# Attention plus a routed expert layer: the sync queue of the expert stage reordered, and the gate and up weights of the next expert loaded in two parts

## The chip, the cores and the metric
The kernel runs on one core of one Trainium2 chip. The metric is the device time of one execution in microseconds (us). Before the change it was 9702.04 us, the median of three runs (9699.02 to 9710.63).

## What is computed
`x` has 16 x 512 = 8192 rows (tokens) of 1024 float32 values. A cross-attention block with a layernorm ahead of it is added to `x`, and then a routed expert layer with a layernorm ahead of it:

```python
routing_weights, selected_experts = top_k(softmax(x2d @ gate_kernel), 8)     # of 32 experts
w0 = ragged_dot(sorted_inputs, gate_proj, group_sizes)      # gate_proj: 32 x 1024 x 384
w1 = ragged_dot(sorted_inputs, up_proj, group_sizes)        # up_proj:   32 x 1024 x 384
inter = silu(w0) * w1
expert_out = ragged_dot(inter, down_proj, group_sizes)      # down_proj: 32 x 384 x 1024
output = sum over the 8 experts of a token of weight * expert_out
```

8192 tokens with 8 experts each give 65,536 rows of expert work. Everything is float32.

## The kernel before
Four stages follow one another: a setup, attention with the routing, a short schedule stage, and the experts (`experts_stage`), which the change touches. The schedule stage groups the rows by expert into **tiles** of up to 512 rows. Each tile belongs to one expert. An expert has several tiles in a row, and the last ones of an expert may be cut to 448 or 384 rows, so that its padding costs less. Here there are 144 tiles (`used`) of 32 experts. Below, "tile t" is the t-th of them, counted from 0, a **short** tile is one of 384 rows, and an expert's weights are loaded only at its first tile: every weight DMA of a later tile carries the condition `CHANGED`, which is 0 there, so it is issued but moves nothing.

Float32 precision comes from splitting each operand into a high and a low part (`..._hi`, `..._lo`) and making three matmuls for each product. For one tile TensorE (`products`) does:
- `gate_up(t, j)` for j = 0, 1, 2: 48 matmuls each (2 matrices, 8 slices c of the 1024 inputs, 3 products; L1576). At j = 0 it waits slice by slice for `xt_lo` (the low part of the input rows, DVE L1484), and before j = 0 and j = 1 for the output rows of the tile before to be out of the banks that it writes (`left_ready`, `right_ready`).
- `down(t, g)`: eight groups of 9 matmuls of 512 columns (L1599). Group g = 2q + n writes one half of output quarter q. The first two groups are done up to their last third while the third part of `h` is being made. In a short tile the two groups of the last quarter are a tiny matmul each (L1626). The last quarter's banks are those of quarter 0.

The other engines run one tile ahead for the weights. In PE's tile t,
- ACT and DVE split the weights of tile t+1 from the single raw buffer `gu_raw` as PE finishes with the old ones: `gate_up_hi(t+1, 0)` and `(t+1, 1)` after j = 1 of tile t, on DVE `gate_up_lo` of the same two (L1490); `(t+1, 2)` only after `left_rows(t, 0)` on ACT and `right_rows(t, 0)` on DVE, which stand ahead of them in program order;
- `left_rows(t, q)` (ACT L1428) and `right_rows(t, q)` (DVE L1514) scale the output rows of quarter q by the routing weight and take them out of PSUM. The one of q = 0 waits for `entry_kept`: the routing weights and row numbers of tile t in `entry_now`. Behind them stand, on both engines, the third weight part, the splitting of the next tile's rows (`x_hi` L1403, `x_lo` L1484) and the later quarters;
- POOL gathers rows for tile t+2 (L1363), then scatters the rows of tile t (L1375).

Program order on ACT after j = 1 of a tile:

```python
gate_up_hi(t, 0); gate_up_hi(t, 1); silu(t - 1, 2)
left_rows(t - 1, 0)
gate_up_hi(t, 2)
for c in range(DC):
    x_hi(t, c)
    if c in ROWS_AFTER:                      # (0, 2, 5)
        left_rows(t - 1, 1 + ROWS_AFTER.index(c))
```

DVE has the same order with `gate_up_lo`, `right_rows` and `x_lo`.

All weights and all table entries are loaded by SyncE, in one order, through one hardware DMA queue. Its four loads are `load_entries(t)` (which rows to gather, `entry_in`, 4 DMAs, L1276), `load_gate_up(t)` (3 MB in 8 DMAs, L1311, after `gulo_ready` says that all three parts of tile t-1 are split), `load_rows(t)` (`entry_now` of tile t, 8 small DMAs, L1287 and L1295, after the scatters of tile t-1 have landed) and `load_down(t)` (1.5 MB in one DMA, L1318, after `dlo_ready` says that the down weights of tile t-1 are split). Before the change the loop runs them as entries(t), gate and up(t-1), rows(t-2), down(t-1).

Of the kernel before, what the change touches and what calls it, by code (L numbers as in the profile page):

```python
# [24 lines left out]
P = 128  # L25
# [11 lines left out]
def wait(eng, sem, value):  # L37

    if isinstance(value, int) and value <= 0:
        return  # L40
    eng.wait_ge(sem, value)  # L41
# [1144 lines left out]
def experts_stage(nc, sb, sem, banks, sched_row, tiles_over, xn_dram, table, gate_proj, up_proj, down_v, out, *,  # L1186
# [12 lines left out]
    QUAD = 32  # L1199
    KQ = P // QUAD  # L1200
# [7 lines left out]
    with mem:  # L1208
        gu_raw = sb(mem, "gu_raw", [P, 2, DC, M], F32)
# [19 lines left out]
        GU_BANK = banks[0:6]  # L1229
        D_BANK = (banks[6:8], banks[0:2], banks[2:4], banks[6:8])  # L1230

        ROWS_AFTER = (0, 2, 5)
        PAIRS = RUNS // 2
        assert PAIRS == DC
# [2 lines left out]
        GATHER_AT = tuple(range(9, GATE_PACES + 1, 3)) + tuple(GATE_PACES + n for n in (2, 4, 5))  # L1237
        assert len(GATHER_AT) == RUNS

        gu_loaded, d_loaded, entry_loaded = sem("gu_loaded"), sem("d_loaded"), sem("entry_loaded")  # L1240
        gathered, scattered = [sem(f"gathered{n}") for n in range(PAIRS)], sem("scattered")
        pace = sem("pace")
        quarter_made, rows_made, entry_kept = sem("quarter_made"), sem("rows_made"), sem("entry_kept")
# [1 line left out]
        guhi_ready, gulo_ready, dhi_ready, dlo_ready = sem("guhi_ready"), sem("gulo_ready"), sem("dhi_ready"), sem("dlo_ready")  # L1245
# [17 lines left out]
        def _(sp):  # L1263
            def hold(semaphore, value):

                sp.wait_ge(semaphore, value)
                sp.sem_inc(fence["sp"], 1)

            def scheduled(t, word, most):
                return sp.value_load(sched_row[0:1, bass.ds(SCHED_WORDS * t + word, 1)], min_val=0, max_val=most)  # L1270

            def load_entries(t):
                first_row = scheduled(t, FIRST_ROW, TABLE_PAD)
                wait(sp, rows_made, t)
                for k in range(KQ):
                    sp.dma_start(entry_in[k * QUAD:(k + 1) * QUAD, :, :].rearrange("r (e m) two -> r e (m two)", m=2),  # L1276
                                 table[bass.ds(first_row, SLOT_ROWS), :].rearrange("(e r m) two -> r e (m two)", r=QUAD, m=2)
                                 ).then_inc(entry_loaded, 16)
# [20 lines left out]
            def expert_of(t):  # L1299

                e = sp.value_load(sched_row[0:1, bass.ds(SCHED_WORDS * t + EXPERT, 1)], min_val=0, max_val=E - 1)
                first = isinstance(t, int) and t == 0
                only = {} if first else {"cond": sp.value_load(sched_row[0:1, bass.ds(SCHED_WORDS * t + CHANGED, 1)], min_val=0, max_val=1)}
                return e, only

            def load_gate_up(t):
                e, only = expert_of(t)
                wait(sp, gulo_ready, MC * t)
                for n, w in enumerate(weights_v):
                    for k in range(KQ):  # L1310
                        sp.dma_start(gu_raw[k * QUAD:(k + 1) * QUAD, n, :, :],  # L1311
                                     w[bass.ds(e, 1), k, :, :, :].rearrange("e r c m -> r (e c) m"), **only
                                     ).then_inc(gu_loaded, 16)

            def load_down(t):
                e, only = expert_of(t)
                wait(sp, dlo_ready, MC * t)
                sp.dma_start(d_raw[:, :, :], down_v[bass.ds(e, 1), :, :, :].rearrange("e p c d -> p (e c) d"), **only  # L1318
                             ).then_inc(d_loaded, 16)

            def tile(t):
                load_entries(t)
                load_gate_up(t - 1)
                load_rows(t - 2)
                load_down(t - 1)
                hold(d_loaded, 16 * t)

            used = used_tiles(sp)
            load_entries(0)
            load_gate_up(0)  # L1330
            load_entries(1)
            load_down(0)
            tile(2)
            tiles_from(sp, 3, used, tile)
            load_entries(used)
            load_gate_up(used - 1)
            load_rows(used - 2)
            load_down(used - 1)
            load_rows(used - 1)
            hold(d_loaded, 16 * used)  # L1340
            hold(entry_loaded, 16 * KQ * (used + 1))
            hold(entry_kept, 16 * 2 * KQ * used)

# [55 lines left out]
        def _(act):  # L1399
# [5 lines left out]
            def gate_up_hi(t, j):  # L1405

                cols = slice(j * P, (j + 1) * P)
                act.wait_ge(gu_loaded, 16 * 2 * KQ * (t + 1))
                wait(act, gu_done, MC * (t - 1) + j + 1)
                act.activation(gu_hi[:, :, :, cols], gu_raw[:, :, :, cols].rearrange("p n c m -> p c n m"), ACT.Copy  # L1410
                               ).then_inc(guhi_ready, 1)
# [19 lines left out]
            def tile(t):  # L1431
# [9 lines left out]
                for c in range(DC):  # L1441
                    x_hi(t, c)
                    if c in ROWS_AFTER:
                        left_rows(t - 1, 1 + ROWS_AFTER.index(c))

            used = used_tiles(act)
# [16 lines left out]
        def _(dve):  # L1463
# [53 lines left out]
            def tile(t):  # L1517
# [18 lines left out]
                for c in range(DC):  # L1536
                    x_lo(t, c)
                    if c in ROWS_AFTER:
                        right_rows(t - 1, 1 + ROWS_AFTER.index(c))

# [126 lines left out]
```

## Time and profile before

| what | value |
|---|---|
| median of three runs | 9702.04 us |
| the profiled execution, span from first to last instruction | 9705.4 us |
| PE busy | 9157.1 us (94%) |
| DVE, ACT, POOL busy | 6503.2, 4465.8, 5282.3 us |
| DMA queue q0 (POOL's gathers and scatters) | 604.72 MB |
| DMA queue q1 (SyncE's) | 308.44 MB |
| mean granted TensorE clock | 0.974 |

The profiled execution has no time of its own apart from its span, 9705.4 us, which is 3.4 us over the median of the runs and inside their spread. The first 3.08 ms are setup, attention and schedule, and the rest, some 6.6 ms, are the 144 tiles. Busy times say how long an engine worked, and only the waits and the order of events say which of them set the end.

### The profile page before, as it was taken

How to read it: one execution, taken by the hardware profiler on the slowest of the kernel's cores; microseconds unless marked ns; L12 is line 12 of the kernel's file. 1: busy time of each engine (PE TensorE's matmuls, PEld its weight loads, DVE VectorE, ACT ScalarE, POOL GpSimd, SP SyncE). 2: the span in 40 equal slices, each digit the busy share in tenths (PEclk: the TensorE clock that was granted, in tenths of full speed). 3: DMA queues.
4: the chain of work that ended last, by engine and by line, in shares of the span. 5: the costliest groups of instructions: out<-in, count | busy, mean ns of one | idle time of the engine just before them, and what ended most of it. 6: DMA issues, size and time to landing. Idle time of an engine off the chain costs nothing.

```text
span 9705.4 us, 172457 instructions
## 1 busy us (share of the span) xinstructions
PE 9157.1 (94%) x44592; PEld 7702.0 (79%) x44593; DVE 6503.2 (67%) x10304; ACT 4465.8 (46%) x7458; POOL 5282.3 (54%) x5081
## 2 busy tenths in 40 slices
PE   7898898898895999999999999999999999999999
PEld 5776777677774888888888888888888888888888
DVE  7888888888885566666655656666666566656565
ACT  6676666676673333333333333333333333333333
POOL 3444444444445566565655656555666555655564
PEclk8999999999997999999999999999999999999999
DMA  2111111111112555555544655555555455555554
GB/s 88 48 53 49 50 51 49 51 53 48 49 51 72 108 112 132 113 112 117 112 106 106 137 109 110 118 111 125 118 112 111 106 118 108 134 109 111 114 123 80
DMA packets 664527, 918.18 MB, mean 95 GB/s; under 512 B 338193, under 2 KB 477457, under 8 KB 663954
## 3 DMA queue, kind: packets, MB, share of 16 engines
q0 software_dynamic: 209920, 604.72, 29.2%
q1 hardware_dynamic: 454162, 308.44, 12.2%
q8 instruction: 168, 2.75, 0.1%
q14 instruction: 277, 2.27, 0.1%
HBM read 1064.79 MB, written 376.45 MB: 148 GB/s over the span
## 4 chain that ended last, share of the span: by engine, by line
PE 60%; DMA 3%; issue 3%; DVE 2%; ACT 1%; SPq 1%; POOL 0%; DVEq 0%; ACTq 0%; POOLq 0%
PE bank L1576 39%; PE bank L1599 21%; DMA gu_raw<-in_L_ffn_up_proj 3%; SPq L1311 1%; DVE gu_lo L1490 0%; ACT xT_hi L1403 0%; DVE xT L1479 0%; ACT gu_hi L1410 0%; DVE h L1502 0%; DVE d_lo L1495 0%; DVE h_lo L1507 0%; DVE h_hi L1505 0%; DVE xT_lo L1484 0%; POOL xg L1363 0%; DVEq L41 0%
## 5 line engine op out<-in xcount | busy, mean ns | idle before, releaser
L1363 POOL DMA_INDIRECT xg<-xn_rows,gather_row x2304 | 2766.7, 1201 | 2086.7 <-PE bank L1576 1310.6
L1576 PE MATMUL bank<-xT_hi,gu_hi 128*128 128x512 f32 (+2 forms) x6912 | 2553.4, 369 | 102.8 <-DVE xT_lo L1484 94.5
L1576 PE MATMUL bank<-xT_lo,gu_hi 128*128 128x512 f32 (+2 forms) x6912 | 2543.2, 368 | 0.0
L1576 PE MATMUL bank<-xT_hi,gu_lo 128*128 128x512 f32 (+2 forms) x6912 | 2543.1, 368 | 0.0
L1421 ACT ACTIVATE gated<-bank 128x512 f32<-128x512 f32 x432 | 258.2, 598 | 3030.0 <-PE bank L1576 2740.1
L1576 PEld LDWEIGHTS bank<-xT_hi,gu_hi 128*128 128x128 f32 x6912 | 1299.2, 188 | 278.6 <-issue 91.5
L1375 POOL DMA_INDIRECT out_rows<-rows_out,entry_now x576 | 1129.0, 1960 | 671.6 <-DVE rows_out L1514 322.5
L1576 PEld LDWEIGHTS bank<-xT_lo,gu_hi 128*128 128x128 f32 x6912 | 1299.7, 188 | 158.9
L1576 PEld LDWEIGHTS bank<-xT_hi,gu_lo 128*128 128x128 f32 x6912 | 1299.1, 188 | 158.9
L1502 DVE TENSOR_TENSOR h<-bank,gated 128x512 f32<-128x512 f32 x432 | 297.6, 689 | 1578.5 <-ACT gated L1421 1133.8
L1599 PE MATMUL bank<-d_hi,h_hi 128*128 128x512 f32 x3162 | 1257.3, 398 | 76.7 <-DVE h_lo L1507 76.7
L1599 PE MATMUL bank<-d_lo,h_hi 128*128 128x512 f32 x3162 | 1244.6, 394 | 0.0
L1599 PE MATMUL bank<-d_hi,h_lo 128*128 128x512 f32 x3162 | 1244.4, 394 | 0.0
L1490 DVE TENSOR_TENSOR gu_lo<-gu_raw,gu_hi 128x2048 fp32r<-128x2048 f32 x432 | 973.3, 2280 | 251.0 <-ACT gu_hi L1410 136.0
L480 ACT ACTIVATE probs<-bank,neg_max 128x512 f32<-128x512 f32 x1024 | 704.9, 688 | 716.6 <-DVE neg_max L605 670.6
L1410 ACT ACTIVATE gu_hi<-gu_raw 128x2048 fp32r<-128x2048 f32 x432 | 809.1, 1907 | 185.3 <-DMA gu_raw<-in_L_ffn_up_proj 171.3
L1514 DVE TENSOR_SCALAR rows_out<-bank,entry_now 128x512 f32<-128x512 f32 x576 | 431.3, 749 | 680.3 <-PE bank L1599 664.8
L1428 ACT ACTIVATE rows_out<-bank,entry_now 128x512 f32<-128x512 f32 x576 | 395.6, 687 | 1003.6 <-PE bank L1599 851.5
L1599 PEld LDWEIGHTS bank<-d_hi,h_hi 128*128 128x128 f32 x3162 | 602.0, 190 | 249.0 <-issue 128.9
L619 DVE TENSOR_TENSOR pT_lo<-bank,pT_hi 128x512 fp32r<-128x512 f32 x1024 | 693.1, 677 | 136.3 <-ACT pT_hi L488 109.8
L605 DVE TENSOR_REDUCE neg_max<-bank 128x1 f32<-128x512 f32 x1024 | 700.6, 684 | 122.4 <-issue 44.3
L1479 DVE STREAM_TRANSPOSE xT<-xg 128x512 f32<-128x512 f32 x1152 | 747.5, 687 | 0.0
(162 smaller groups left out, 14769.3 us busy)
## 6 DMA issues: line engine op xcount, KB each, us to landing
gu_raw<-in_L_ffn_gate_proj SPq DMA_DIRECT2D x576, 384.0 KB
gu_raw<-in_L_ffn_up_proj SPq DMA_DIRECT2D x576, 384.0 KB
d_raw<-in_L_ffn_down_proj SPq DMA_DIRECT2D x144, 1536.0 KB
xg<-xn_rows,gather_row POOLq DMA_INDIRECT x2304
x_t<-in_x SPq DMA_DIRECT2D x64, 512.0 KB, 4.4
inv_wide<-inverse_sums SPq DMA_DIRECT2D x512, 64.0 KB
out_rows<-x SPq DMA_DIRECT2D x64, 512.0 KB, 5.0
xn_rows<-xn SPq DMA_DIRECT2D x64, 512.0 KB
```

The costliest lines, as they stand in the source:

```text
L480: act.activation(probs[h % 4][:, :], S_BANK[h % 2][:, :], ACT.Exp, bias=neg_max[:, h:h + 1], accum_out=row_sum[:, h:h + 1]).then_inc(exp_r ...
L605: dve.tensor_reduce(neg_max[:, h:h + 1], S_BANK[h % 2][:, :], AX.X, ALU.max, negate=True).then_inc(max_ready, 1)
L619: dve.tensor_tensor(pT_lo[g % 2][:, :, k, :], PT_BANK[h % 2][:, :].rearrange("p (c t) -> p c t", c=TC), pT_hi[g % 2][:, :, k, :].bitcast(F ...
L1363: pool.indirect_dma_start(out=xg[:, m, :], out_offset=None, in_=quarter_rows, in_offset=bass.IndirectOffsetOnAxis(ap=gather_row[:, m:m + 1 ...
L1375: pool.indirect_dma_start(out=out, out_offset=bass.IndirectOffsetOnAxis(ap=entry_now[:, q, 0:1], axis=0), in_=rows_out[:, q, :], in_offset ...
L1410: act.activation(gu_hi[:, :, :, cols], gu_raw[:, :, :, cols].rearrange("p n c m -> p c n m"), ACT.Copy).then_inc(guhi_ready, 1)
L1428: act.activation(rows_out[:, q, 0:512], D_BANK[q][0][:, :], ACT.Copy, scale=entry_now[:, q, 1:2].bitcast(F32)).then_inc(left_ready, 1)
L1479: dve.transpose(xT[:, :, 2 * pair * QUAD:2 * (pair + 1) * QUAD].rearrange("p c (m r) -> p m c r", r=QUAD), xg[:, 2 * pair:2 * pair + 2, :] ...
L1490: dve.tensor_tensor(gu_lo[:, :, :, cols], gu_raw[:, :, :, cols].rearrange("p n c m -> p c n m"), gu_hi[:, :, :, cols].bitcast(F32), ALU.su ...
L1514: dve.tensor_scalar(rows_out[:, q, 512:1024], D_BANK[q][1][:, :], entry_now[:, q, 1:2].bitcast(F32), None, ALU.mult).then_inc(right_ready, 1)
L1576: last = nc.tensor.matmul(bank[:, 0:cols], w[:, c, n, j * P:(j + 1) * P], v[:, c, 0:cols], start=(c == 0 and w is gu_hi and v is xT_hi), s ...
L1599: last = nc.tensor.matmul(D_BANK[q][n][:, 0:cols], v[:, k, q * P:(q + 1) * P], w[:, k, n * 512:n * 512 + cols], start=(k == ks[0] == 0 and ...
```

## The change
On SyncE the loop body now runs entries(t+1), down(t-1), the first part of gate and up(t), rows(t-2), the second part of gate and up(t). The first part is columns 0 to 255 of both matrices (j = 0 and 1) and waits only until the first two parts of tile t-1 are split. The second is columns 256 to 383 (j = 2) and waits for all three. Each part has its own semaphore, and ACT waits for the one that it needs. Each part has 8 DMAs, so a tile has 16 where it had 8. Rows of 1536 bytes become rows of 1024 and 512 bytes. The start and the end of the queue are rewritten to fit. PE, DVE, ACT and POOL keep their order.

```diff
+        EARLY = MC - 1
+        GU_PARTS = (slice(0, EARLY * P), slice(EARLY * P, M))
...
-        gu_loaded, d_loaded, entry_loaded = sem("gu_loaded"), sem("d_loaded"), sem("entry_loaded")
+        gu_loaded, d_loaded, entry_loaded = (sem("gu_early"), sem("gu_late")), sem("d_loaded"), sem("entry_loaded")
...
-            def load_gate_up(t):
+            def load_gate_up(t, part):
+
                 e, only = expert_of(t)
-                wait(sp, gulo_ready, MC * t)
+                wait(sp, gulo_ready, MC * t if part else MC * (t - 1) + EARLY)
                 for n, w in enumerate(weights_v):
                     for k in range(KQ):
-                        sp.dma_start(gu_raw[k * QUAD:(k + 1) * QUAD, n, :, :],
-                                     w[bass.ds(e, 1), k, :, :, :].rearrange("e r c m -> r (e c) m"), **only
-                                     ).then_inc(gu_loaded, 16)
+                        sp.dma_start(gu_raw[k * QUAD:(k + 1) * QUAD, n, :, GU_PARTS[part]],
+                                     w[bass.ds(e, 1), k, :, :, GU_PARTS[part]].rearrange("e r c m -> r (e c) m"), **only
+                                     ).then_inc(gu_loaded[part], 16)
...
             def tile(t):
-                load_entries(t)
-                load_gate_up(t - 1)
+                load_entries(t + 1)
+                load_down(t - 1)
+                load_gate_up(t, 0)
                 load_rows(t - 2)
-                load_down(t - 1)
-                hold(d_loaded, 16 * t)
+                load_gate_up(t, 1)
+                hold(d_loaded, 16 * (t - 1))
 
             used = used_tiles(sp)
             load_entries(0)
-            load_gate_up(0)
+            for part in range(2):
+                load_gate_up(0, part)
             load_entries(1)
             load_down(0)
-            tile(2)
+            load_entries(2)
+            for part in range(2):
+                load_gate_up(1, part)
+            load_entries(3)
+            load_down(1)
+            load_gate_up(2, 0)
+            load_rows(0)
+            load_gate_up(2, 1)
             tiles_from(sp, 3, used, tile)
...
             def gate_up_hi(t, j):
 
                 cols = slice(j * P, (j + 1) * P)
-                act.wait_ge(gu_loaded, 16 * 2 * KQ * (t + 1))
+                act.wait_ge(gu_loaded[0 if j < EARLY else 1], 16 * 2 * KQ * (t + 1))
```

The order of SyncE before, in the loop: the end of the table loads of one tile, the down weights, and the end of the pass. L1303 is part of `expert_of`, L1295 of `load_rows`, L1318 of `load_down`.

```order
L1295 DMA entry_now<-slot_table 32x2
L1301 TENSOR_LOAD sched_row
L1301 ISA x2
L1303 TENSOR_LOAD sched_row
L1303 ISA x2
L1318 ISA [waits dlo_ready]
L1318 DMA d_raw<-in_L_ffn_down_proj 128x3x1024
L1266 REGISTER_ALU
L1256 UNCONDITIONAL_BRANCH [waits d_loaded]
```

Here nothing that waits for a weight split of the following tile stands ahead of the table loads of tile t-2: they come before the down weights of tile t-1 and before the pass that loads gate and up of tile t.

The order of SyncE now, at the same loads: L1314 is `load_gate_up`, here its first part for tile t, and L1289 is `load_rows` of tile t-2.

```order
L1314 DMA gu_raw<-in_L_ffn_gate_proj 32x8x256
L1314 DMA gu_raw<-in_L_ffn_up_proj 32x8x256 x4
L1272 ISA
L1272 TENSOR_LOAD sched_row
L1272 ISA x2
L41 REGISTER_ALU
L1289 ISA [waits scattered]
L1289 DMA entry_now<-slot_table 32x3x2
```

The table loads of tile t-2 have moved behind the down weights of tile t-1, the entries of tile t+1 and the 8 DMAs of the first part of tile t.

The wait ahead of that first part on SyncE now (L1321 is `load_down`, L1305 part of `expert_of`):

```order
L1321 ISA [waits dlo_ready]
L1321 DMA d_raw<-in_L_ffn_down_proj 128x3x1024
L1303 ISA
L1303 TENSOR_LOAD sched_row
L1303 ISA x2
L1305 ISA
L1305 TENSOR_LOAD sched_row
L1305 ISA x2
L41 REGISTER_ALU
L1314 ISA [waits gulo_ready]
L1314 DMA gu_raw<-in_L_ffn_gate_proj 32x8x256
```

So whatever stands behind `[waits gulo_ready]`, the table loads among it, cannot be issued before the second part of tile t-1 is split.

## Rows read from the trace of the kernel before
**Rows 1.** The page: the chain that ended last, share of the span by engine.

```profile
PE 60%; DMA 3%; issue 3%; DVE 2%; ACT 1%; SPq 1%; POOL 0%; DVEq 0%; ACTq 0%; POOLq 0%
```

**Rows 2.** Waits from 3200 us on: who <- for whom: us in total, times, longest.

```profile
PE bank L1599 <- DVE h_lo L1507: 70.3, 18, 6.2
```

**Rows 3.** Chain of waits, a full tile and a change of expert: start us, us, what.

```profile
4154.77 32.64 PE bank L1576 x144
...
4281.32 23.64 DMA gu_raw<-in_L_ffn_up_proj
```

**Rows 4.** Timeline of PE there: start us, us, what [idle before <- releaser].

```profile
4313.41 0.61 PE L1599 MATMUL bank<-d_hi,h_hi 128*128 128x512 f32 x1 [4.45 <-DVE h_lo L1507]
...
4317.35 0.39 PE L1599 MATMUL bank<-d_lo,h_hi 128*128 128x512 f32 x1
```

**Rows 5.** First gate matmul of tiles 25, 26 and 27: timeline of PE.

```profile
4241.48 0.39 PE L1576 MATMUL bank<-xT_hi,gu_hi 128*128 128x384 f32 x1
...
4280.10 0.39 PE L1576 MATMUL bank<-xT_hi,gu_hi 128*128 128x384 f32 x1
...
4324.78 0.45 PE L1576 MATMUL bank<-xT_hi,gu_hi 128*128 128x512 f32 x1
```

**Rows 6.** Table loads and gate/up loads on SyncE: timeline, tiles 25 and 26.

```profile
4253.04 1.87 SPq L1287 DMA_DIRECT2D entry_now<-slot_table  x4
4255.76 2.50 SPq L1295 DMA_DIRECT2D entry_now<-slot_table  x4
...
4276.58 2.11 SPq L1311 DMA_DIRECT2D gu_raw<-in_L_ffn_gate_proj  x4
4278.78 6.46 SPq L1311 DMA_DIRECT2D gu_raw<-in_L_ffn_up_proj  x4
...
4320.17 1.16 SPq L1311 DMA_DIRECT2D gu_raw<-in_L_ffn_gate_proj  x4
4321.42 0.90 SPq L1311 DMA_DIRECT2D gu_raw<-in_L_ffn_up_proj  x4
```

**Rows 7.** Short tile 25: timeline of DVE, and of ACT (the last row).

```profile
4262.96 4.45 DVE L1490 TENSOR_TENSOR gu_lo<-gu_raw,gu_hi 128x2048 fp32r<-128x2048 f32 x2
...
4273.95 2.35 DVE L1490 TENSOR_TENSOR gu_lo<-gu_raw,gu_hi 128x2048 fp32r<-128x2048 f32 x1 [1.06 <-issue]
4276.82 0.74 DVE L1514 TENSOR_SCALAR rows_out<-bank,entry_now 128x512 f32<-128x512 f32 x1
4277.48 1.28 DVE L1484 TENSOR_TENSOR xT_lo<-xT,xT_hi 128x512 fp32r<-128x512 f32 x2
...
4271.42 0.69 ACT L1428 ACTIVATE rows_out<-bank,entry_now 128x512 f32<-128x512 f32 x1 [3.19 <-issue]
```

**Rows 8.** Full tile 23: DVE, ACT, and the first matmul of tile 24.

```profile
4180.22 4.45 DVE L1490 TENSOR_TENSOR gu_lo<-gu_raw,gu_hi 128x2048 fp32r<-128x2048 f32 x2
...
4191.23 0.69 ACT L1428 ACTIVATE rows_out<-bank,entry_now 128x512 f32<-128x512 f32 x1 [3.19 <-PE bank L1599]
...
4203.83 0.33 PE L1576 MATMUL bank<-xT_hi,gu_hi 128*128 128x384 f32 x1
```

**Rows 9.** First use of a small load: timeline of SyncE, then DVE.

```profile
3042.74 2.75 SPq L1276 DMA_DIRECT2D entry_in<-slot_table  x4
...
3052.16 8.99 SPq L1276 DMA_DIRECT2D entry_in<-slot_table  x4
...
3046.89 0.23 DVE L1471 TENSOR_SCALAR gather_row<-entry_in,quarter_no 128x16 int32<-128x16 int32 x1 [9.61 <-DMA entry_in<-slot_table]
```

**Rows 10.** Stretches: us, busy of PE, PEld, DVE, ACT, POOL, PEclk, DMA share, GB/s.

```profile
4267.40:4276.30 8.90, 8.90 (x40) 7.09 (x39) 4.93 (x7) 5.23 (x7) 7.07 (x7) 1.00 0.29 89
4301.00:4312.00 11.00, 7.96 (x42) 7.10 (x41) 5.71 (x5) 4.20 (x3) 7.18 (x7) 1.00 0.94 282
4313.60:4317.00 3.40, 3.40 (x9) 2.62 (x9) 0.63 (x1) 1.94 (x2) 0.00 (x0) 0.50 0.17 5
```

**Rows 11.** Gate/up matmuls of the short tiles, grouped by shape.

```profile
L1576 PE MATMUL bank<-xT_hi,gu_hi 128*128 128x384 f32 x2352 | 794.5, 338 | 12.2 <-DVE xT_lo L1484 12.2
```

More of the change, by code:

```diff
@@ L1321, in tile @@
             def tile(t):
-                load_entries(t)
-                load_gate_up(t - 1)
+                load_entries(t + 1)
+                load_down(t - 1)
+                load_gate_up(t, 0)
                 load_rows(t - 2)
-                load_down(t - 1)
-                hold(d_loaded, 16 * t)
+                load_gate_up(t, 1)
+                hold(d_loaded, 16 * (t - 1))
             used = used_tiles(sp)
             load_entries(0)
-            load_gate_up(0)
+            for part in range(2):
+                load_gate_up(0, part)
             load_entries(1)
             load_down(0)
-            tile(2)
+            load_entries(2)
[6 more added lines that the diff above has]
+            load_gate_up(2, 1)
             tiles_from(sp, 3, used, tile)
-            load_entries(used)
-            load_gate_up(used - 1)
+            load_down(used - 1)
             load_rows(used - 2)
-            load_down(used - 1)
             load_rows(used - 1)
             hold(d_loaded, 16 * used)
+            for part in range(2):
+                hold(gu_loaded[part], 16 * 2 * KQ * used)
             hold(entry_loaded, 16 * KQ * (used + 1))
```

## The prediction
> **What bounds the kernel now.** I read the page first: the chain that ended last is PE for 60% of the span, and the only DMA in it is the load of gate and up weights [rows 1]. PE is the bound, so what counts is where PE stands still. The waits from 3200 us on show one cause: PE waits for the last part of `h` in 18 places, 70.3 us in all [rows 2]. The chain at one of them shows why [rows 3]: the gate and up weights of the next expert land at 4304.96, ACT can only then split them, its `silu` and DVE's `h` stand behind that, and PE gets going at 4313.41 after 4.45 us of standing still [rows 4]. Then it is slow for a while: a matmul is recorded with 0.61 us where later ones have 0.39, and the granted clock in that stretch is 0.50, so 1.2 instead of 2.4 GHz, after the engine stood still [rows 4, 10]. Tile 26, where this happens, lasts 44.68 us, and the equally short tile 25 ahead of it 38.62 [rows 5]. So one stall costs 6.1 us where its gap is 4.45. The 70.3 us of gaps cost about 70.3 x 6.1 / 4.45 = 96 us, and the starts of all tiles added up give 102. I take 100 us: all that an earlier load of the weights can bring back in the steady part.
>
> **What the first part gains.** The load starts at 4276.58 today, 0.28 us after the third `gu_lo` ends at 4276.30, and with the change it may start after the second, at 4267.41, 9.2 us sooner and with 2 MB instead of 3 [rows 6, 7]. Today it lands at 4304.96 and that is about 6 us late, so it is first wanted near 4299. Today 3 MB take 28.4 us from first issue to landing (4276.58 to 4304.96 [rows 3, 6]). Two thirds of that, 19 us, would be 4286.6. The second part is used after the next `left_rows`, 17 us later. Both are hidden: **-100 us**. At the start of the stage the first split waits for 2 MB instead of 3. But gathers end it a few us later anyway, so I take -4 us there (bounds 0 and -9, a third of the 28.4 us).
>
> **What is moved past what.** The price is on the other loads of that queue. `load_rows(t-2)`, the 8 small DMAs that ACT and DVE need before they may take output rows out, was issued early in its tile (4253.04, used at 4271.42 [rows 6, 7]). Now it stands behind `gulo_ready` of the first part and behind that part's 8 DMAs. Both lie within the same tile. Counted from the end of the second `gu_lo` (G):
>
> - Tiles where the following weights do not change: 0.28 us from G to the first issue, 2.15 for 8 issues that move nothing (4320.17 to 4322.32), 0.85 for the table look-up that precedes a load (4254.91 to 4255.76), 5.22 for the 8 small issues (4253.04 to 4258.26), 1.4 from the last issue to first use, as DVE shows it (3045.49 to 3046.89) [rows 6, 9]. Sum: **G + 9.9**.
> - Tiles before a change: the 8 DMAs are real and the small ones queue behind 2 MB. Rows 9 show small loads held up behind weights: 4 issues take 8.99 us where they usually take under 3. DMA was 0.29 busy in the 8.9 us after G and moved 282 GB/s when full [rows 10], so 2 MB at 0.7 x 282 = 197 GB/s take 10.6 us. With about 1 us to the first byte, 1.4 to use and another for the small packets this gives **G + 14**. The lower bound is the issue alone, 0.28 + 4.3 + 0.85 + 5.22 + 1.4 = 12.1. With today's slow issue (8.65 us) it is 16.4, and with today's rate for the whole load (19 us) about 20.6.
>
> When is it wanted? In short tile 25 `left_rows` starts at 4271.42, which is G + 4.0 [rows 7]. In full tile 23 it is G + 6.6 (4184.67 to 4191.23 [rows 8]); for a tile of 448 rows I take G + 5.4, between the two. So **every** tile gets its rows late: by 5.9, 3.3 or 4.5 us without a weight change, by 10.0, 7.4 or 8.6 with one.
>
> What of this reaches PE? Behind `left_rows(t, 0)` stand the third weight split, `x_lo` of slice 0 and the second `right_rows`, which ends 6.14 us later (4277.56), and PE may not start the next tile before. In tile 25 it starts at 4280.10, a slack of 2.5 us. In full tile 23 the same point leaves 6.5 us (4191.23 + 6.14 = 4197.4, start 4203.83) [rows 5, 7, 8]. After that point DVE still has 5.9 us of work to the last slice (7 slices at 0.64, 2 `right_rows` at 0.74 [rows 7]), while PE gets to that slice after 21 matmuls, 4.8 us at 0.23 (32.64 / 144 [rows 3]) or 3.6 at 0.17, that is 384/512 of it. The delay that is free is therefore slack + 4.8 (3.6) - 5.9:
>
> - Full tile without a weight change: free up to 5.4 (full tile next) or 4.2 (short next), delay 3.3: **0**. For 448 rows 4.5 against 4.2: 0.3 in 7 tiles, 2 us.
> - Short tile without a weight change. There are 49 short tiles (2352 matmuls of that shape, 48 in each tile [rows 11]). 22 of them are the last of an expert, with a full tile next: 5.9 - 1.4 = 4.5 us each, **99 us**. 10 have another short tile next: 5.9 - 0.25 less the 0.95 that a short tile after a short one loses already (38.62 against 37.65, from 4203.83 to 4241.48 [rows 5, 8]), 4.7 each, **47 us**.
> - Tiles before a weight change (31, by the lengths of the blocks): 15 short before short, 10.0 - 0.25 - 0.95 = 8.8 and 0.5 for the slow clock after a gap of 7.5 us, which is mostly hidden since DVE sets the pace there: **140 us**. 5 of 448 before short, 8.6 - 4.2 = 4.4: **22 us**. 11 full ones, 7.4 against 5.4, 4.8 or 4.2 by what follows (4, 5, 2 of them): 8 + 13 + 6 = **27 us**.
>
> New stalls: 2 + 99 + 47 + 140 + 22 + 27 = 337 us. The rest costs nothing: eight more issues a tile (2.15 us) and the entries and down weights that move ahead lie on SyncE, which issues for some 10 us of a tile's 38.6 and otherwise waits, as it does for `gu_lo` until 4276.58 [rows 5, 6]. Without that cover it would be 144 x 2.15 = 310 us. The scatters start some 2 to 7 us later behind POOL's gathers, whose rows are used most of a tile later.
>
> Sum against the profiled span: 9705.4 - 100 - 4 + 337 = 9938. That execution stands 3.4 us over the median, so I predict 9702 + 233 = **9935 us**.
>
> A rule of the Trainium skill is weighed here. In the trace, with gathers, scatters and weights at once, 3 MB take 28.4 us, 111 GB/s of the 282 that the engines reach [rows 3, 6, 10]. DMA: Bandwidth & Descriptors, section Queues, rings and completion order, says that each DMA engine takes turns between the queues by packets, and reads one ring in order. By it the weights could get less than the 0.7 that I give them beside gathers, and the sum would then be that of the third rival, 10,138 us.
>
> **The rivals.**
> 1. *The table rows are not late, and the change does what it is for.* Were small DMAs not held by the weights, or `gu_lo` of part two early enough, only -104 would be left: 9702 - 104 = 9598 us, faster. For it: the weight stall is real and goes in full. It decides if the small loads are usable by G + 4 to 6.5. Against it: 2.15 + 0.85 + 5.22 us of issue after G are 8.2 already without any queueing. 0.04. A neighbouring rule: the same section of DMA: Bandwidth & Descriptors says that completion is not in order within an issuing engine. By it small DMAs might finish before the weights do, but they are issued no sooner.
> 2. *A draw.* The rows are late, but the tiles before a weight change are no worse than others: 31 delays fall to those of the first list. Then new stalls are 99 + 47 + 2 + 15 x 4.7 + 2 = 221 us, and 9819 us is still slower. A draw needs 32 + 15 short tiles to lose 2.2 us each instead of 4.5 to 9. The gap at their start alone is 5.9 - 2.5 = 3.4. 0.03.
> 3. *The weights go as slowly as today.* G + 20.6 in 31 tiles, 6.6 us more each: +205, 10,138 us. For it: contention with gathers. Against it: today's load runs beside the scatters, and these now wait for the rows themselves. 0.06.
> 4. *Half of the price*, 9819 us as worked out under 2, the weight changes no worse than other tiles: 0.08.
>
> **The numbers.** The forecast has 0.79, the rivals 0.04, 0.03, 0.06 and 0.08. Its own bounds: landing at 12.1 and 9.0 instead of 14 and 9.9 gives 337 - 57 - 29 = 251, 9849 us; issue at 16.4 gives +74, 10,009 us. The range reaches down to the second rival's 9819 and up by some clock loss: 9815 to 10,040. A measurement of this kernel tells 0.2% (19 us) from no change. Slower 0.93, within 0.2% 0.03, faster 0.04.
>
> **What would show it.** Right: PE no longer waits for `h_lo` at L1599 in the steady part; ACT `rows_out` (L1440 now) waits for a DMA of `entry_now` in nearly every tile; PE waits for `xT_lo` or the output rows at the first gate matmul, about 3.4 us after each short tile and 7 us before a weight change; short tiles last 42 to 48 us instead of 38, full ones stay at 49.2; the clock shows more stretches of 0.5, at tile starts. Wrong: `rows_out` of quarter 0 starts within 4 to 6.6 us of the second `gu_lo`, as before, or PE waits for weights still.

## The result and the profile after

The changed kernel takes 10,069.12 us (median of 5 runs, 10,060.24 to 10,073.94) against 9702.04, a ratio of 1.0375 with a 95% interval of 1.0363 to 1.0388. It is 367 us slower. The prediction had 9935 us, +233, and a range up to 10,040. The direction and the mechanism came out as forecast, the size did not, and the time lies above the range.

The first place to look is the list of waits of the changed kernel from 3200 us on (who <- for whom: us in total, times, longest).

```profile
ACT rows_out L1440 <- DMA entry_now<-slot_table: 1201.2, 129, 16.1
DVE rows_out L1526 <- DMA entry_now<-slot_table: 956.1, 129, 14.2
...
PE bank L1588 <- DVE rows_out L1526: 220.8, 55, 5.1
...
PE bank L1638 <- ACT rows_out L1440: 70.3, 15, 5.0
...
PE bank L1611 <- ACT rows_out L1440: 40.8, 16, 3.6
...
PE bank L1588 <- DVE xT_lo L1496: 11.1, 28, 0.5
```

ACT and DVE now wait for the table rows in 129 tiles. Before, no such row was among the waits. PE's wait for `h_lo` (18 times, 70.3 us [rows 2]) is gone. In its place PE waits 55 times for output rows at the start of a tile, 15 times ahead of the tiny matmul of a short tile's last quarter, and 16 times ahead of the last quarter of a longer one: 345 us of standing still where it was 86. The page's chain has changed with it:

```profile
PE 43%; issue 10%; DVE 6%; SPq 5%; DMA 3%; ACT 2%; DVEq 0%; POOL 0%; ACTq 0%; POOLq 0%
PE bank L1588 31%; PE bank L1611 12%; DMA entry_now<-slot_table 2%; DVE gu_lo L1502 2%; SPq L1314 2%; ACT gu_hi L1422 1%; DVE xT L1491 1%; SPq L1272 1%; SPq L1289 1%; DVE rows_out L1526 1%; SPq L1297 1%; DVE d_lo L1507 1%; DVE xT_lo L1496 1%; DVE h_hi L1517 0%; ACT gated L1433 0%
```

PE's part is down from 60% [rows 1] to 43%, and the queue of SyncE (SPq) stands in it with 5%.

Short tile 25 again, whose second next tile has a new expert. First SyncE's timeline in the changed kernel, for this tile (from 4327) and for tile 24 ahead of it (from 4282), where the weights do not change:

```profile
4282.92 1.14 SPq L1314 DMA_DIRECT2D gu_raw<-in_L_ffn_gate_proj  x4
4284.15 0.88 SPq L1314 DMA_DIRECT2D gu_raw<-in_L_ffn_up_proj  x4
4286.53 1.86 SPq L1289 DMA_DIRECT2D entry_now<-slot_table  x4
4289.45 2.65 SPq L1297 DMA_DIRECT2D entry_now<-slot_table  x4
...
4327.37 2.11 SPq L1314 DMA_DIRECT2D gu_raw<-in_L_ffn_gate_proj  x4
4329.57 1.88 SPq L1314 DMA_DIRECT2D gu_raw<-in_L_ffn_up_proj  x4
4332.48 1.84 SPq L1289 DMA_DIRECT2D entry_now<-slot_table  x4
4335.29 2.38 SPq L1297 DMA_DIRECT2D entry_now<-slot_table  x4
```

DVE's timeline, the same two tiles:

```profile
4278.18 4.45 DVE L1502 TENSOR_TENSOR gu_lo<-gu_raw,gu_hi 128x2048 fp32r<-128x2048 f32 x2
...
4322.63 4.45 DVE L1502 TENSOR_TENSOR gu_lo<-gu_raw,gu_hi 128x2048 fp32r<-128x2048 f32 x2
...
4343.94 0.75 DVE L1526 TENSOR_SCALAR rows_out<-bank,entry_now 128x512 f32<-128x512 f32 x1 [14.13 <-DMA entry_now<-slot_table]
...
4349.26 0.74 DVE L1526 TENSOR_SCALAR rows_out<-bank,entry_now 128x512 f32<-128x512 f32 x1
```

And ACT's, for the first use of the rows in tile 24 and in tile 25:

```profile
4293.32 0.69 ACT L1440 ACTIVATE rows_out<-bank,entry_now 128x512 f32<-128x512 f32 x1 [9.87 <-PE bank L1611]
...
4343.93 0.69 ACT L1440 ACTIVATE rows_out<-bank,entry_now 128x512 f32<-128x512 f32 x1 [16.03 <-DMA entry_now<-slot_table]
```

The second `gu_lo` ends at 4282.63 and 4327.08. That is G. The rows are used at G + 10.7 in tile 24 and at G + 16.9 in tile 25, where it was G + 4.0 [rows 7]. In tile 25 the last small DMA is issued by 4337.67, 6.3 us before that use, and it waits behind the weights: by the times of the single packets in the trace, the first packet of a table row moves at 4340.93, when all but the last of the weights have moved (they end at 4341.64), and the last one ends at 4341.88. It is so in all 31 tiles before a weight change: 93 to 98% of the weight packets start ahead of the first table packet. Over all tiles the first use lies at G + 16.4 to 17.1 in these 31 (median 16.6), at G + 10.3 to 11.3 in other tiles of 384 and 448 rows (median 10.8), and at G + 9.7 to 10.1 in other full ones (median 9.8). Only tile 142, at the rewritten end of the queue, has its rows at G + 4.0. PE after that, in its timeline:

```profile
4344.67 0.69 PE L1638 MATMUL bank<-d_hi,h_hi 128*128 128x128 f32 x2 [4.91 <-ACT rows_out L1440]
4350.29 0.68 PE L1588 MATMUL bank<-xT_hi,gu_hi 128*128 128x384 f32 x1 [4.93 <-DVE rows_out L1526]
4350.77 0.53 PE L1588 MATMUL bank<-xT_lo,gu_hi 128*128 128x384 f32 x1
...
4356.48 0.33 PE L1588 MATMUL bank<-xT_hi,gu_lo 128*128 128x384 f32 x1
```

Two gaps of 4.9 us, and then slow matmuls. By its first matmuls (4299.64 and 4350.29) tile 25 lasts 50.7 us; before it lasted 38.6 [rows 5]. The stretches of the same kernel: the first is that of the weights' transfer, the second that of the slow matmuls (us, busy of PE, PEld, DVE, ACT, POOL, PEclk, DMA share, GB/s).

```profile
4328.30:4341.60 13.30, 11.46 (x50) 8.89 (x48) 1.44 (x3) 0.00 (x0) 5.13 (x5) 1.00 1.07 217
...
4350.30:4356.00 5.70, 5.70 (x18) 5.70 (x19) 5.70 (x11) 4.83 (x7) 4.47 (x3) 0.50 1.07 212
```

The clock records after 3200 us hold 376 us at 0.50 (1.2 GHz) in 55 stretches, where it was 93 us in 18.

What each kind of tile lasts more than before, from the starts of all 144 tiles (so for the first 143):

| tiles | number | us more each | us in all |
|---|---|---|---|
| short, before a weight change | 15 | 11.25 | 168.7 |
| 448 or 512 rows, before a weight change | 16 | 4.3 | 69.0 |
| short, last of its expert | 22 | 1.19, on top of the 102.4 us of weight stalls that are gone | 26.2 |
| full, first of its expert | 31 | 1.50 (2.11 in the 22 behind a short tile, 0.02 in the other 9) | 46.6 |
| short, others | 11 | 4.34 | 47.7 |
| all others | 48 | about 0.2 | 10.4 |

Together 368.7 us. Of the last row 9.1 us lie in 9 tiles of 448 and 512 rows that are the last of an expert. With the 102.4 us that came back, the new stalls are 471 us, where the prediction had 337.

### The profile page after: what moved, and what is told of

It is laid out like the page before. It is cut to its first block, busy times and chain, and to the rows that moved or that the text cites. A ratio compares the mean times of both kernels' runs of the same rounds, so it can differ in the third digit from the quotient of the medians.

```text
span 10071.9 us, 176762 instructions
## 1 busy us (share of the span) xinstructions
PE 9252.4 (92%) x44592; PEld 7763.5 (77%) x44593; DVE 6474.7 (64%) x10304; ACT 4436.6 (44%) x7458; POOL 5108.5 (51%) x5081
## 4 chain that ended last, share of the span: by engine, by line
PE 43%; issue 10%; DVE 6%; SPq 5%; DMA 3%; ACT 2%; DVEq 0%; POOL 0%; ACTq 0%; POOLq 0%
PE bank L1588 31%; PE bank L1611 12%; DMA entry_now<-slot_table 2%; DVE gu_lo L1502 2%; SPq L1314 2%; ACT gu_hi L1422 1%; DVE xT L1491 1%; SPq L1272 1%; SPq L1289 1%; DVE rows_out L1526 1%; SPq L1297 1%; DVE d_lo L1507 1%; DVE xT_lo L1496 1%; DVE h_hi L1517 0%; ACT gated L1433 0%
## 5 line engine op out<-in xcount | busy, mean ns | idle before, releaser
L1375 POOL DMA_INDIRECT xg<-xn_rows,gather_row x2304 | 2735.4, 1187 | 1960.7 <-PE bank L1588 1303.1
L1588 PE MATMUL bank<-xT_hi,gu_hi 128*128 128x512 f32 (+2 forms) x6912 | 2600.8, 376 | 324.8 <-DVE rows_out L1526 222.2
L1588 PE MATMUL bank<-xT_lo,gu_hi 128*128 128x512 f32 (+2 forms) x6912 | 2581.7, 374 | 0.0
L1588 PE MATMUL bank<-xT_hi,gu_lo 128*128 128x512 f32 (+2 forms) x6912 | 2579.3, 373 | 0.0
L1588 PEld LDWEIGHTS bank<-xT_hi,gu_hi 128*128 128x128 f32 x6912 | 1327.6, 192 | 522.4 <-DVE xT_lo L1496 261.0
L1387 POOL DMA_INDIRECT out_rows<-rows_out,entry_now x576 | 991.2, 1721 | 1334.5 <-DVE rows_out L1526 1219.7
L1588 PEld LDWEIGHTS bank<-xT_lo,gu_hi 128*128 128x128 f32 x6912 | 1327.6, 192 | 161.4
L1588 PEld LDWEIGHTS bank<-xT_hi,gu_lo 128*128 128x128 f32 x6912 | 1325.3, 192 | 164.0
```

What stands on the lines that cost most here:

```text
L1375: pool.indirect_dma_start(out=xg[:, m, :], out_offset=None, in_=quarter_rows, in_offset=bass.IndirectOffsetOnAxis(ap=gather_row[:, m:m + 1 ...
L1387: pool.indirect_dma_start(out=out, out_offset=bass.IndirectOffsetOnAxis(ap=entry_now[:, q, 0:1], axis=0), in_=rows_out[:, q, :], in_offset ...
L1588: last = nc.tensor.matmul(bank[:, 0:cols], w[:, c, n, j * P:(j + 1) * P], v[:, c, 0:cols], start=(c == 0 and w is gu_hi and v is xT_hi), s ...
```

## The experiments

Every ratio below is of runs on the same chip to the kernel before, which took 9693 to 9710 us (medians) in these comparisons.

**1. The rows put ahead.** The order of the changed kernel with one line moved, in the loop and in the start:

```diff
                 load_down(t - 1)
-                load_gate_up(t, 0)
                 load_rows(t - 2)
+                load_gate_up(t, 0)
                 load_gate_up(t, 1)
```

> The changed kernel with one move: the table loads of tile t-2 stand ahead of the first part of gate and up, not behind it. Theory (the late table rows are the whole loss, the two-part load is the gain): the rows are in time again, PE no longer waits for weights, about 9600 us (9702 - 100 - 4). Rival A (the loads themselves cost: 16 DMAs of 1024 and 512 bytes for 8 of 1536, started beside the gathers): the time stays over 9800 us although the rows are in time. Rival B (both, in part): between 9620 and 9800 us.

Measured: 9596.3 us, ratio 0.989 (0.9873 to 0.9906). Of PE's waits from 3200 us on only these are left:

```profile
PE bank L1588 <- DVE xT_lo L1496: 12.2, 26, 0.5
PE bank L1588 <- issue: 0.2, 1, 0.2
```

The rows are used at G + 4.0 in short and 6.6 in full tiles, as before the change; in tile 25, whose second `gu_lo` ends at 4238.34, on ACT:

```profile
4242.34 0.69 ACT L1440 ACTIVATE rows_out<-bank,entry_now 128x512 f32<-128x512 f32 x1 [3.18 <-PE bank L1611]
```

So the place of this one load makes all of the loss, some 470 us, and the rest of the change is a gain of 1.1%. Rival A, that the loads themselves cost, is out. SyncE's timeline of tile 25 shows how rows and weights both come in time:

```profile
4224.62 1.83 SPq L1289 DMA_DIRECT2D entry_now<-slot_table  x4
4227.31 2.63 SPq L1297 DMA_DIRECT2D entry_now<-slot_table  x4
4238.64 2.13 SPq L1314 DMA_DIRECT2D gu_raw<-in_L_ffn_gate_proj  x4
4240.86 1.88 SPq L1314 DMA_DIRECT2D gu_raw<-in_L_ffn_up_proj  x4
4247.52 2.11 SPq L1314 DMA_DIRECT2D gu_raw<-in_L_ffn_gate_proj  x4
4249.72 6.61 SPq L1314 DMA_DIRECT2D gu_raw<-in_L_ffn_up_proj  x4
```

The rows go out 14 us ahead of the first part of the new expert's weights, which starts 0.3 us after its `gu_lo`. The second part follows at 4247.52, and its last four issues take 6.61 us, where those of the first part took 1.88. Nothing that is due soon stands behind them.

**2. The split in the old order.** Against the kernel before, the loop alone (the start and the end of the queue are changed to match):

```diff
             def tile(t):
                 load_entries(t)
-                load_gate_up(t - 1)
+                load_gate_up(t - 1, 0)
+                load_gate_up(t - 1, 1)
                 load_rows(t - 2)
                 load_down(t - 1)
                 hold(d_loaded, 16 * t)
```

> The old order of the sync queue, entries(t), gate and up(t-1), rows(t-2), down(t-1), with gate and up loaded in the two parts of the change. Theory: the split alone brings the whole gain, since the rows of a tile still stand ahead of the weights two tiles on: about 9600 us, as rows_first. Rival A (small pieces cost): over 9700 us. Rival C (the gain needs the down weights to be loaded ahead): only part of the 100 us comes, 9640 us or more, with waits for d_raw or gu_raw left.

Measured: 9597.1 us, ratio 0.9897 (0.988 to 0.9913), with 13 us of PE waits left:

```profile
PE bank L1584 <- DVE xT_lo L1492: 12.2, 26, 0.5
...
PE bank L1584 <- DVE rows_out L1522: 1.0, 1, 1.0
```

The split alone brings the whole gain. Rival C is out: nothing of it needed the down weights ahead. Here the table rows of tile t-2 do stand behind both parts of the weights of tile t-1, and it does no harm, because these weights were let go a tile earlier: those of tile 27 are issued from 4232.30 on, the rows of tile 26 behind them from 4259.09 on, and their first use is at 4274.60. So what hurts is not any large load ahead, but one that is let go shortly before the small one is due.

**3. The new order alone,** rows ahead, weights whole:

```diff
             def tile(t):
-                load_entries(t)
-                load_gate_up(t - 1)
-                load_rows(t - 2)
+                load_entries(t + 1)
                 load_down(t - 1)
-                hold(d_loaded, 16 * t)
+                load_rows(t - 2)
+                load_gate_up(t)
+                hold(d_loaded, 16 * (t - 1))
```

> The new order with the rows put ahead of the weights, and gate and up whole, 8 DMAs of 1536-byte rows, after the old wait for all three parts. Theory: the load starts when it did before (third gu_lo), so nothing is gained or lost: 9702 us within 15, with the 18 waits for h_lo as before. Rival C (the earlier down weights take the weight load's way or clear it): more than 20 us away from 9702 to either side.

Measured: 9717.3 us, ratio 1.0021 (1.0012 to 1.0031). The waits for `h_lo` are all there:

```profile
PE bank L1602 <- DVE h_lo L1510: 79.8, 21, 5.8
```

The theory said 9702 within 15. The median lies 15.3 above that, and against the kernel before on the same chip the ratio makes it 12 to 30 us, so the theory missed by a little, and rival C (over 20 us away) is neither met nor out. 21 waits of 79.8 us in all instead of 18 of 70.3 [rows 2] are 9.5 us of it; the tiles' starts put 12.9 us more into the tiles, 10 of them in the short last tiles of an expert. Why three more waits arise was not looked into. The new order gains nothing by itself.

**4. The wait without the queueing.** The rows go out after the wait for the second `gu_lo`, but ahead of the eight DMAs:

```diff
                 e, only = expert_of(t)
                 wait(sp, gulo_ready, MC * t if part else MC * (t - 1) + EARLY)
+                if rows_of is not None:
+                    load_rows(rows_of)
                 for n, w in enumerate(weights_v):
```

The loop and the start pass the tile of the rows to this function in place of their own call of `load_rows`.

> The changed kernel, but the rows are issued right after the wait for the second gu_lo and ahead of the 8 DMAs of the first part. So they keep the wait and lose the queueing behind 2 MB and the 2.15 us of issues. Theory: rows usable at G + 7.7 us in all tiles; 3.7 us late in short tiles, whose gap at the next tile's start is then 1.2 us, too short for the clock to fall; 22 x 2.3 + 25 x 2.5 = 113 us of new stall, 9598 + 113 = 9711 us, and at most 5 stretches of half clock after 3200 us. Rival (the wait alone makes the loss, whatever is queued ahead): near 10069 us. Rival (only the 2 MB ahead matter): near 9600 us.

Measured: 9695.2 us, ratio 0.9998 (0.9988 to 1.0008). Waits from 3200 us on:

```profile
ACT rows_out L1440 <- DMA entry_now<-slot_table: 756.4, 139, 7.6
...
DVE rows_out L1526 <- DMA entry_now<-slot_table: 492.3, 139, 5.7
...
PE bank L1588 <- DVE rows_out L1526: 50.9, 47, 1.9
```

The rows are used at G + 7.4 to 8.4 in short tiles, median 7.5 (7.7 expected). PE's 47 waits are those of 47 short tiles, 1.1 us each (1.2 expected), and only 2 stretches of half clock are left. This kernel takes 99 us more than experiment 1, where 113 were expected. So the wait costs about 100 us, which is what the split gains, and what stands between the wait and the rows (the eight issues, their bytes and a table look-up) costs the other 374. Both rivals, the wait alone (10,069) and the 2 MB alone (9600), are out.

**5. and 6. Without the bytes.** In the kernel before and in the changed one, gate and up are loaded for tile 0 alone. Later DMAs are issued and move nothing:

```diff
-            def expert_of(t):
+            def expert_of(t, changed_at=None):
...
-                only = {} if first else {"cond": sp.value_load(sched_row[0:1, bass.ds(SCHED_WORDS * t + CHANGED, 1)], min_val=0, max_val=1)}
+                only = {} if first else {"cond": sp.value_load(sched_row[0:1, bass.ds(SCHED_WORDS * (t if changed_at is None else changed_at) + CHANGED, 1)], min_val=0, max_val=1)}
...
             def load_gate_up(t):
-                e, only = expert_of(t)
+                e, only = expert_of(t, 1)
```

The condition is then always that of tile 1, which is 0, so all tiles compute with the gate and up weights of the first expert. The down weights are loaded as before.

> The kernel before, with gate and up loaded for tile 0 only: the DMAs of later tiles are issued but move nothing (all tiles use the first expert's gate and up weights, so that part of the computation is changed). Theory (the stalls for these weights cost 100 us, gap and slow clock together): 9602 us, and no wait for h_lo after 3200 us. Rival: only the gaps count, 70 us: 9632 us.

> The changed kernel, with gate and up loaded for tile 0 only, in the same way (that part of the computation is changed). It takes the queueing behind 2 MB away and leaves the wait and 8 issues. Theory: rows usable at G + 10 us in all tiles, 47 short tiles lose 4.4 us each and 22 full tiles behind them 1.9 more for the slow clock: 9602 + 207 + 42 = 9851 us. Rival (only the weights' bytes ahead of the rows hurt): near 9602 us. Rival (the clock plays no part): 9602 + 207 = 9809 us or less.

Measured: 9604.5 us for the kernel before, ratio 0.9894 (0.9877 to 0.991), and 9895.9 us for the changed one, ratio 1.0198 (1.0179 to 1.0216). The first has no wait for `h_lo` left. Of PE's waits from 3200 us on there are only these:

```profile
PE bank L1576 <- DVE xT_lo L1484: 12.2, 26, 0.5
PE bank L1576 <- issue: 3.4, 1, 3.4
```

So the weight stalls cost 9702 - 9604 = 98 to 106 us (against its own comparison of 9710). The gaps alone, 70 us, are not enough. The second shows what the wait and eight issues cost without any bytes of these weights: 9896 - 9604 = 291 us. Its waits:

```profile
ACT rows_out L1440 <- DMA entry_now<-slot_table: 1115.8, 139, 10.9
...
PE bank L1588 <- DVE rows_out L1526: 213.8, 47, 5.1
```

47 short tiles with 4.5 us of gap each. In its tiles of 448 and 512 rows nothing is lost except in the first of an expert. The bytes are worth the rest, 10,069 - 9896 = 173 us. By the starts of tiles 155 of it lie in the 31 tiles before a weight change and 9 in the longer tiles behind them. The changed kernel without these bytes came 45 us above the 9851 expected: the full tiles behind short last ones lose 44 us together, near the 42 expected, and the short tiles 5.5 us each and not 4.4. The rival of the bytes alone (9602) is out. That of no part for the clock (9809 or less) cannot be judged by this number, since the excess lies in the short tiles; the next experiment tries it.

**7. The clock held up.** The changed kernel with 8 more matmuls ahead of the last quarter and 8 at the end of a short tile, out of constant operands into a free bank:

```diff
+                def filler():
+                    for _ in range(8):
+                        nc.tensor.matmul(GU_BANK[2 * MC - 2][:, :], fill_r[:, 0:P], fill_r[:, :],
+                                         start=True, stop=True)
...
+                        if g == OUT_GROUPS - NH:
+                            filler()
                         empty_group(t, g)
+                if cols == LESS_TWO:
+                    filler()
```

> The changed kernel with 16 matmuls of 512 columns more in each short tile, into a free bank, with operands of their own: 8 ahead of the wait for the last quarter's banks, 8 at the tile's end. They take 3.6 us of PE where PE stands still for 4 to 13 us, and add no wait. Theory (after gaps over some 3.3 us the clock falls, and that is the term I set too low, 283 us more at half clock than before): half-clock stretches after 3200 us fall from 55 to 25 or fewer, and the time by 50 to 110 us, to 9960 to 10,020 us. Rival (the slow clock is hidden behind DVE's slices, and the loss is later landings alone): the stretches fall and the time stays at 10,069 within 15 us, or rises.

Measured: 10,041.6 us, ratio 1.034 (1.0322 to 1.0357), 27.5 us less than the changed kernel (34 by the ratios). The gaps at the starts of tiles shrink, as they should:

```profile
PE bank L1596 <- DVE rows_out L1531: 63.2, 52, 3.3
```

The half-clock stretches fall from 55 to 30 (25 or fewer expected) and their time from 376 to 160 us, but the gain is half of the least that I expected. 216 us less of half clock are worth 27.5 us, one eighth, where a PE that is bound by its own work would get back one half. The tiles say why. The first 48 matmuls of tile 27, which stands behind a short last tile, in the changed kernel and in this one (the columns of the stretches above):

```profile
4395.00:4408.50 13.50, 13.49 (x48) 10.94 (x49) 11.24 (x17) 4.89 (x7) 7.27 (x5) 0.80 0.81 138
```

```profile
4382.60:4394.30 11.70, 11.56 (x48) 8.96 (x49) 11.26 (x17) 4.92 (x7) 7.97 (x5) 1.00 0.88 144
```

In the 22 such tiles the 49th matmul starts 13.05 us after the first, and 11.69 us with the filler. This is 1.4 us each, and their loss falls from 2.11 to 0.75 us, 30 us in all.

In 10 short tiles behind a short one, all at full clock with the filler, it starts after 10.14 us instead of 10.62: 0.5 us each. There DVE's last `x_lo` slice is ready 5.3 us after the tile's first matmul at either clock. PE is there to use it after 5.4 us at full clock and after 5.9 in the changed kernel, so DVE's pace hides most of the slow clock. The short tiles as a whole lose as much as before or a little more (11.20 against 11.25 before a weight change, 4.90 against 4.34 before another short one). That does not prove their clock to be free, for two reasons. Their rows are used 0.3 to 0.4 us later after G with the filler (16.9 and 11.1 against 16.6 and 10.8, why was not tried), which eats the gain. And the boundaries behind the 15 short tiles before a weight change keep much of their half clock (6.8 us each instead of 11.2).

So neither theory stands as it was put: the clock has a price, 30 us behind short last tiles and an estimated 12 at the starts of short tiles (0.5 us in 25), and it is the smaller part of the loss.

**8. Half of the bytes ahead.** The rows are issued between the gate and the up DMAs of the first part:

```diff
                 for n, w in enumerate(weights_v):
+                    if n == 1 and rows_of is not None:
+                        load_rows(rows_of)
                     for k in range(KQ):
```

The loop and the start pass the tile of the rows, as in experiment 4.

> The changed kernel with the rows issued between the 4 gate and the 4 up DMAs of the first part: 1 MB ahead of them instead of 2. Theory (the rows wait for the bytes issued ahead of them): 1 MB drains in half of the 13.3 us, so the issues and the bytes end together, rows usable at about G + 10.5 us before a weight change (16.6 with 2 MB) and at G + 9 elsewhere, where 4 issues are saved. Every short tile then loses some 4 us, which is 9840 us within 30. Rival (the rows are held until the whole load has landed, however little stands ahead): G + 16 to 17 before a weight change, and 10,000 us or more.

Measured: 9873.9 us, ratio 1.0185 (1.0167 to 1.0202), 34 us above the 9840 expected and 4 outside its bounds. The rows are used at G + 11.1 to 12.2 before a weight change and at G + 8.9 to 10.6 in the other tiles (10.5 and 9 expected). SyncE's timeline of tile 25, before a weight change (its second `gu_lo` ends at 4279.32), and DVE's first use of the rows:

```profile
4279.61 2.10 SPq L1316 DMA_DIRECT2D gu_raw<-in_L_ffn_gate_proj  x4
4283.22 1.60 SPq L1289 DMA_DIRECT2D entry_now<-slot_table  x4
4285.68 2.91 SPq L1297 DMA_DIRECT2D entry_now<-slot_table  x4
4288.69 1.84 SPq L1316 DMA_DIRECT2D gu_raw<-in_L_ffn_up_proj  x4
```

```profile
4290.85 0.75 DVE L1526 TENSOR_SCALAR rows_out<-bank,entry_now 128x512 f32<-128x512 f32 x1 [8.80 <-DMA entry_now<-slot_table]
```

The last small DMA is issued by 4288.59, its last packet ends 0.85 us later, and DVE begins at 4290.85. Over the 31 tiles the last table packet ends 0.85 us (median) after the last issue, where it was 3.9 us in the changed kernel. So the issues and not the bytes now set it. The first table packet moves when 43 to 50% of the weights have moved. Nothing holds the rows until the whole load has landed. What is issued ahead of them is what they wait for.

## Why the prediction was right in kind and wrong in size

**Right.** The bound and the gain: 100 us of weight stalls, measured 98 to 106 (experiment 5) and 102.4 by tiles, gone in full. That the rows of each tile become late, and that this costs more than the split gains: experiments 1 and 4 show it directly. The delay in full tiles without a weight change (G + 9.9, measured 9.8; the 31 that are neither first nor last of an expert are within 0.04 us of before), the 448-row ones (0), and the short ones before another short one (4.7 predicted, 4.34 measured, in 11 tiles and not 10). All four rivals are out: the faster case, the draw and the half price by more than 240 us, and the third by 70, since the rows came at G + 16.6 and not 20.6. Two slips in the rivals changed nothing: the third adds up to 10,140, and the 221 us of the second and fourth are two thirds of 337 and not half. The 4 us at the start of the stage stay open: tile 0 began between 3065 and 3079 us in the traces of the kernels here, with the same stages ahead of it, and that hides them.

**Wrong, first step: "2 MB at 0.7 x 282 = 197 GB/s take 10.6 us ... this gives G + 14".** The transfer took 13.3 us, 158 GB/s, while all queues together moved 217, and the use came at G + 16.6. So the share of 0.7 was right (158 of 217 is 0.73), and the total was not. The 282 was read from a stretch in which 1.57 of 3.10 MB were down weights, in packets of 4096 bytes, while the first part of gate and up now moves in packets of 1024. After 3200 us such a packet took 80 ns on average in the changed kernel, one of 1536 bytes 100 ns in the kernel before, and one of 4096 bytes (down weights) 166 ns in the changed kernel and 183 in the one before: 12.8, 15.4 and 22 to 25 bytes per ns. That the packet size is the cause was not tried by itself; the gathers beside them differ too. The 2 MB were 2048 packets, as many as the 3 MB had been.

The upper bound with today's slow issue, 16.4, happened to be near it, for another reason: the issues took 4.1 us and not 8.65, and the transfer made it late. The bytes cost 173 us by experiment 6, where the prediction's own terms give 189 - 15 x 4.7 - 2 = 117. So this step is short by 56 us.

The Trainium skill, DMA: Bandwidth & Descriptors, section Queues, rings and completion order, was weighed there: each DMA engine takes turns between the queues by packets and reads one ring in order. The trace agrees with the second half: the table packets of tile 25 moved from 4340.93 on, behind the weights issued ahead of them. What was drawn from the first half, less than 0.7 for the weights, did not come: they had 0.73.

**Wrong, second step: "Short tile without a weight change ... 4.5 us each", 146 us for 32 tiles, 220 for 47 if no tile had a change.** Experiment 6 has 291. Two things make the 71 us.

The rows are used at G + 10.6 to 11.6 there in short tiles (median 11.1) instead of 9.9, and the gap ahead of the next tile is 4.5 us instead of 3.4, 54 us in 47 tiles. In tile 24 of the changed kernel the table look-up ahead of the rows takes 1.5 us instead of 0.85 (4285.03 to 4286.53) and the issues 5.6 instead of 5.2. I had taken the 0.85 from the pause inside the table loads. Ahead of them it is 1.5 us in short tiles without a weight change and 1.0 in full ones, where the eight issues are shorter too (1.86 us against 2.12). In short tiles all this falls where POOL is gathering and DVE works; what slows SyncE was not tried.

The other thing is the price of the first full tile behind a short last one: 2.0 us in each of 22 tiles, where 1.1 us of DVE's pace had been counted, 20 us in all. Experiment 7 shows 1.4 of the 2.0 us to be the slow clock. The starts of short tiles behind short ones cost 5 us less than forecast.

**The clock, "0.5 for the slow clock ... mostly hidden".** For short tiles that was right (0.5 us measured), and for the full tiles behind them it was left out. It is 30 us, a part of the 71. Of the 134 us that are missing by the starts of tiles (471 - 337), the two steps make 56 + 71 = 127, and the other 7 lie between the two ways of counting: by the times of the runs the new stalls are 291 + 173 = 464 us.

**The range.** Its upper end, 10,040, took in the late landing (10,009) and some 31 us for the clock. It left out that the rows could be an extra microsecond late in every short tile, the 54 us above. The large terms that were off all pointed the same way. The late landing was in the range as a bound, but for a reason (slow issue) that did not occur, so that it was near was luck.

## What to carry to other kernels

A small load that is due soon must not be queued behind a wait for something else or behind a large load, even if the large one is the one that stalls the kernel today: here one line's place is worth 470 us, 9596 against 10,069. A large load ahead that was let go a tile earlier did no harm (experiment 2). When a step is put earlier in a queue, list what comes after it and when each of those is wanted, in the shortest tile, not the average one. And split a load by the buffer part that comes free first: that alone gained 1.1% here, with the old order.

## What the runs showed of the hardware beyond that

- After 47 gaps of up to 1.9 us PE kept its full clock nearly everywhere (2 stretches at half, experiment 4). After gaps of 4.1 us and more in the changed kernel it ran at 0.50 for a while, and in the kernel before after each of its gaps of 3.3 to 6.2. In between there is no sharp line: in the changed kernel a gap of 3.2 us left the clock full, and with the filler some of less than 3 us had half clock at them. But 216 us less of half clock were worth only 27.5 us, in part since PE was waiting for slices from DVE at those times.
- A DMA whose condition is 0 is not free: after 3200 us eight of them take SyncE 1.8 to 2.4 us in these kernels. Eight real ones take 4.1 us and more: 4.1 to 5.5 in the changed kernel, 8.65 for the 3 MB of [rows 6], and up to 15.5 in experiments 1 and 4. What sets that was not tried.
- Rows of 1024 and 512 bytes instead of 1536 cost nothing that shows in the time: experiment 2 is at the time of the kernel that loads gate and up only once (9597 and 9604 us). In the packets it shows: 12.8 bytes per ns at 1024 bytes and 15.4 at 1536.
